# A two-layer attention kernel: an exponential released earlier, pieces of the MLP's input made between gelus, six first scores moved up

## The reference

```python
q = gconv1x1(bn1(x), qw); kv = grid_sample(bn1(x), grid + tanh(offsets(q)) * 4)      # 64 keys per head
bias = mlp3(sign(pos) * log1p(|pos|))                                              # 2 -> 64 -> 64 -> 1
x = x + conv1x1(softmax(q k^T * scale + bias) v, out_w) + out_b
x = x + conv1x1(gelu(conv1x1(bn2(x), mlp_w1) + mlp_b1), mlp_w2) + mlp_b2           # 256 -> 1024 -> 256
q, k, v = x W_qkv + b_qkv                                                          # second layer
x = x + softmax(q k^T * scale) v W_out + b_out                                     # 16 heads of 1024 x 1024
```

## Time and profile before

| | us |
|---|---|
| median of three runs (lowest, highest) | 1280.26 (1278.66, 1280.81) |
| the profiled execution's own time | 1279.23 |
| its span, first to last instruction | 1277.3 |
| PE busy | 1224.8 (96%) |
| DVE busy | 800.3 (63%) |
| ACT busy | 834.7 (65%) |
| POOL busy | 695.0 (54%) |

### The profile page before, as it was taken

How to read it: one execution, slowest core, us unless ns; L and a number is a source line. 1 busy time by engine, 2 the same in 40 slices (tenths; PEclk the granted TensorE clock), 3 DMA queues, 4 the chain that set the end, 5 groups by cost and what they waited for, 6 DMA issues and landing times.

```text
span 1277.3 us, 25474 instructions
## 1 busy us (share of the span) xinstructions
PE 1224.8 (96%) x10548; PEld 539.0 (42%) x10548; DVE 800.3 (63%) x1026; ACT 834.7 (65%) x1024; POOL 695.0 (54%) x391
## 2 busy tenths in 40 slices
PE   6499999999999999999999999898999899999998
PEld 4333333333333333333333333656886555555554
DVE  6766666666666666666666665554332677777773
ACT  4678777777777777887778877447442355555552
POOL 3366666666666666666666665250000056666664
PEclk9589999999999999999999999998999999999999
DMA  2340110111011011011001100000004413222212
GB/s 76 97 145 2 34 34 1 35 34 31 4 34 34 1 35 35 1 35 34 25 11 34 34 1 2 1 1 1 1 1 165 172 38 71 61 61 61 60 36 78
DMA packets 22507, 51.67 MB, mean 40 GB/s; under 512 B 5622, under 2 KB 10870, under 8 KB 22264
## 3 DMA queue, kind: packets, MB, share of 16 engines
q1 hardware_dynamic: 20084, 43.74, 12.2%
q10 hardware_dynamic: 2308, 6.30, 2.0%
HBM read 36.64 MB, written 11.15 MB: 37 GB/s over the span
## 4 chain that ended last, share of the span: by engine, by line
PE 90%; DVE 4%; ACT 2%; DMA 1%; POOL 1%; issue 1%; SPq 0%; POOLq 0%; DVEq 0%; ACTq 0%
PE ps L999 34%; PE ps L1008 18%; PE ps L1203 6%; PE ps L1233 5%; PE ps L990 5%; PE ps L1244 5%; PE ps L1136 4%; PE ps L1121 3%; PE ps L1165 2%; PE ps L1254 2%; PE ps L1298 1%; PE ps L1179 1%; DVE big L711 1%; PE ps L1021 1%; PE ps L1024 1%
## 5 line engine op out<-in xcount | busy, mean ns | idle before, releaser
L999 PE MATMUL ps<-big,w 64*64 64x512 f32 x2736 | 324.0, 590 | 0.0
L558 ACT ACTIVATE big<-ps 128x1024 f32<-128x1024 f32 x172 | 176.2, 1024 | 87.7 <-PE ps L999 87.7
L770 DVE TENSOR_SCALAR big<-big 128x1024 f32<-128x1024 f32 x171 | 118.7, 694 | 169.2 <-POOL big L447 169.2
L447 POOL TENSOR_TENSOR big<-qpad 128x1024 f32<-128x1024 f32 x86 | 164.3, 1911 | 96.6 <-DVE big L770 28.7
L764 DVE TENSOR_TENSOR big<-qpad,ps 128x1024 f32<-128x1024 f32 x171 | 207.4, 1213 | 1.2 <-PE ps L969 1.2
L447 POOL TENSOR_TENSOR big<-qpad,V 128x1024 f32<-128x1024 f32 x85 | 162.4, 1910 | 80.2 <-DVE ring L770 28.8
L558 ACT ACTIVATE big<-ps,vec 128x1024 f32<-128x1024 f32 x172 | 190.6, 1108 | 0.1
L863 DVE TENSOR_REDUCE amax<-ps 128x1 f32<-128x1024 f32 x128 | 154.0, 1210 | 43.2 <-PE ps L1203 42.4
L999 PEld LDWEIGHTS ps<-big,w 64*64 64x64 f32 x2736 | 98.0, 133 | 151.8 <-issue 85.5
L1008 PE MATMUL ps<-big,w3s 128*32 128x512 f32 x1376 | 160.4, 595 | 0.0
L999 PE MATMUL ps<-ring,w 64*64 64x512 f32 x1360 | 160.4, 588 | 0.0
(11 more groups left out here) (179 smaller groups left out, 1680.8 us busy)
## 6 DMA issues: line engine op xcount, KB each, us to landing
raw<-s_f SPq DMA_DIRECT2D x32, 512.0 KB, 5.9
h1l<-k_d SPq DMA_DIRECT2D x33, 128.0 KB, 3.6
h1h<-q_d ACTq DMA_DIRECT2D x33, 128.0 KB, 4.2
X<-in_x SPq DMA_DIRECT2D x2, 1024.0 KB, 6.1
q_d<-XN SPq DMA_DIRECT2D x4, 512.0 KB, 3.1
k_d<-XN SPq DMA_DIRECT2D x4, 512.0 KB, 3.4
q_d<-big SPq DMA_DIRECT2D x4, 512.0 KB, 3.6
k_d<-big SPq DMA_DIRECT2D x4, 512.0 KB, 3.8
```

Source lines behind the costliest of these rows:

```text
L447: pool.tensor_tensor(h1[m % HRING].rearrange("p (y a b) -> p y a b", y=2, b=W), u.unsqueeze(2).to_broadcast(shape), a[:, :, HALF // W * hf ...
L558: act.activation(h2[m % H2RING], z2[m % ZRING], ACT.Relu, bias=v("cb2") if m % 2 else 0.0).then_inc(h2_ready, 1)
L770: dve.tensor_scalar(h1[m % HRING], h1[m % HRING], 0.0, None, ALU.max).then_inc(h1_ready, 1)
L999: last = pe.matmul(z2[m % ZRING][CH * y:CH * (y + 1), HALF * x:HALF * (x + 1)], w2[CH * x:CH * (x + 1), :], h1[m % HRING][CH * x:CH * (x + ...
```

## The change

1. ACT's wait for the last burst moves from ahead of the loop over u to the copies of u = 2 to 9. The exponentials of u = 0 and 1 no longer wait for it.
2. ACT makes the pieces of block 0 of the MLP's input before the gelus, and those of block n + 1 before the third step of block n. DVE's `split_x` follows the same way: the two of block 0 between the additions to X, the two of block n + 1 ahead of the fourth step of block n.
3. `along(0)` to `along(5)` (`EARLY` = 6) move into `project3(5)` to `project3(7)`: one between the two halves, one behind the value. These six share one pair of PSUM banks, 4 and 5, so each waits for the maximum of the one before. Values use banks 6 and 7 alone. On DVE two maxima stand ahead of each remainder of n = 5 to 7. `along(6)` waits for the remainder of n = 6, `along(7)` for that of n = 7, and `value(8)` to `value(15)` stand between `along(6)` to `along(13)`.

```diff
+EARLY = 6
@@ along_pair
+            if x < EARLY:
+                return 2
@@ scalar
-            act.wait_ge(l3_done, PAIRS * G // BURST)
             for u in range(G + 2):
                 if 2 <= u < 10:
                     n = u - 2
+                    act.wait_ge(l3_done, PAIRS * G // BURST)
...
-            for n in range(T):
+            def normed_x(n):
                 for ct in range(CT):
...
+            normed_x(0)
             for i in range(T * FT):
                 f = i % FT
+                if f == 2 and i // FT < T - 1:
+                    normed_x(i // FT + 1)
                 act.wait_ge(hid_ready, i + 1)
...
             for n in range(NK, 2 * NK):
                 save_value(n)
-            max_high(0)
+                if turning(n - NK + EARLY):
+                    max_high(0)
@@ vector
-                    if r > 0:
-                        split_x(r - 1)
-            split_x(CT * T - 1)
+                    if r in (2, 3):
+                        split_x(r - 2)
...
             for i in range(T * FT):
+                if i % FT == 3 and i // FT < T - 1:
+                    for ct in range(CT):
+                        split_x(CT * (i // FT + 1) + ct)
...
             for n in range(2 * T):
+                for x in range(2 * (n - 2 * T) + EARLY, 2 * (n - 2 * T) + EARLY + 2):
+                    if x >= 0:
+                        maxes(x)
                 dve.wait_ge(f_hi, n + 1)
...
-                if x < SLOTS:
+                if EARLY <= x < SLOTS:
                     maxes(x)
@@ tensor, project3
+                early = 2 * (n - 2 * T) + EARLY
                 for hf in range(2):
                     for kt in range(CT):
...
+                    if hf == 0 and early >= 0:
+                        along(early)
                 last.then_inc(p_ready, 1)
+                value(n)
+                if early >= 0:
+                    along(early + 1)
@@ value
-                elif n >= 4:
-                    pe.wait_ge(vv_saved, n - 3)
+                elif n >= 2:
+                    pe.wait_ge(vv_saved, n - 1)
-                    last = pe.matmul(bank(4 + n % 4)[:, 0:C], ...
+                    last = pe.matmul(bank(6 + n % 2)[:, 0:C], ...
@@ along
-                if 2 <= x < AHEAD_MAX and not turning(x - 1):
+                if x == 0:
+                    pe.wait_ge(bo_saved, 1)
+                elif x < EARLY:
+                    pe.wait_ge(mx_ready, x)
+                elif x < EARLY + 2:
+                    pe.wait_ge(f_lo, 2 * T - (x == EARLY))
+                elif x < AHEAD_MAX and not turning(x - 1):
                     pe.wait_ge(mx_ready, x if turning(x) else x - 1)
@@ tensor, main
             for n in range(2 * T):
                 project3(n)
-                value(n)
-            pe.wait_ge(f_lo, 2 * T)
-            for x in range(AHEAD_MAX):
-                if x < NK:
-                    value(NK + x)
+            for x in range(EARLY, AHEAD_MAX):
+                value(NK + x - EARLY)
```

More of the change, by code:

```diff
@@ L621, in save_value @@
                 act.wait_ge(vv_ready, n + 1)
-                act.activation(V[:, NH * b:NH * (b + 1), jt, :], bank(4 + n % 4)[:, 0:C].rearrange("p (n d) -> p n d", d=D),
+                act.activation(V[:, NH * b:NH * (b + 1), jt, :], bank(6 + n % 2)[:, 0:C].rearrange("p (n d) -> p n d", d=D),
                                ACT.Identity).then_inc(vv_saved, 1)
@@ L1166, in project3 @@
                                          X[:, CT * b + kt, HALF * hf:HALF * (hf + 1)], start=(kt == 0), stop=(kt == CT - 1))
+                    if hf == 0 and early >= 0:
+                        along(early)
                 last.then_inc(p_ready, 1)
+                value(n)
+                if early >= 0:
+                    along(early + 1)
             def value(n):
                 b, jt = n // NK, n % NK
-                if n == 1:
-                    pe.wait_ge(bo_saved, 1)
-                elif n == 2:
+                if n == 0:
                     pe.wait_ge(x2_ready, CT * T)
-                elif n >= 4:
-                    pe.wait_ge(vv_saved, n - 3)
+                elif n >= 2:
+                    pe.wait_ge(vv_saved, n - 1)
                 for kt in range(CT):
-                    last = pe.matmul(bank(4 + n % 4)[:, 0:C], X[:, CT * b + kt, P * jt:P * (jt + 1)], wv[:, kt, 2, :],
+                    last = pe.matmul(bank(6 + n % 2)[:, 0:C], X[:, CT * b + kt, P * jt:P * (jt + 1)], wv[:, kt, 2, :],
                                      start=(kt == 0), stop=(kt == CT - 1))
@@ L1187, in along @@
                     pe.wait_ge(st_in[n % HEADS3], 96 * (n // HEADS3 + 1))
-                if 2 <= x < AHEAD_MAX and not turning(x - 1):
+                if x == 0:
[5 more added lines that the diff above has]
+                elif x < AHEAD_MAX and not turning(x - 1):
                     pe.wait_ge(mx_ready, x if turning(x) else x - 1)
-                elif 2 <= x < AHEAD_MAX:
+                elif x < AHEAD_MAX:
                     pe.wait_ge(m_lo, 1)
-                elif x < 2:
-                    pass
                 elif turning(x):
```

## The result

| | before | after |
|---|---|---|
| median of four runs side by side (us) | 1279.81 (1278.66 to 1280.81) | 1265.33 (1263.76 to 1267.42) |
| profiled execution, own time / span | 1279.23 / 1277.3 | 1263.76 / 1262.0 |

The ratio is 0.9888, 95% interval 0.9869 to 0.9908: 14.5 us faster, against a forecast of 1266.0.

A forecast was written before the change was run, and what follows sets the result against it. PE, on 90% of the span, was taken to lose time by waiting or running at its lower clock in three places. Gains 3.0 + 6.5 + 4.7 = 14.2 us gave a median of 1266.0, range 1262.5 to 1272.0.

The forecast's parts named there:

- Part 1: Last burst's end: earlier exponential removes PE's wait of 2.20 and the slow clock behind it; 3.0 us, bounds 2.2 and 3.9.
- the second head was late next: Behind the last burst: with the first wait gone, the second head's normalization comes at 811.7, 2.7 before the old 814.43.
- Part 2: Start of the MLP: pieces made between the gelus let `mlp_out(0)` follow `hidden(2)` without a wait; 6.5 us, bounds 3.6 and 6.5.
- both its terms: Start of the MLP: PE's wait of 3.56 us goes, and 2.94 of slow matmuls behind it if that wait lowered the clock.
- The room in front of `mlp_out(2)`: MLP's third step: delayed third gelu lets `mlp_out(2)` start at 880.3, PE comes at 880.4; 0.1 us of room.
- Part 3: Second attention's start: six early scores end the fourteenth maximum at 1018.9 instead of 1023.6; 4.7 us, bounds 3.0 and 5.9.
- The walk up to the first `across`: PE and DVE timed from `along(0)` at 990.0: last remainder ends at 1007.5, fourteenth maximum at 1018.9.
- the upper bound: First `across`, second attention: the early scores' upper bound of 5.9, with some 0.9 more if the clock level holds.
- The sum: Whole kernel: 3.0 + 6.5 + 4.7 = 14.2 us gained, giving a median of 1266.0.
- Rival C: Early scores gain nothing: head 0's operands land some 5 us later, or PE loses what DVE wins; 1270.7, chance 0.08.
- Rival D: Early scores: short PE waits drop the clock, 42.4 us for what takes 25.2; 1283.2, slower than before, chance 0.05.

The follow-up runs named there:

- the filled wait: Kernel before the change, with 14 extra matmuls whose result nobody reads put into PE's wait ahead of `mlp_out(0)`: 1276.61 us, ratio 0.9985.
- part 3 alone: Kernel before the change, with only the six early scores (`EARLY` = 6) and all that belongs to them: 1271.37 us, ratio 0.9948.
- head 0's loads earlier: Changed kernel with head 0's query loads issued behind n = 2, heads 1 and 2 behind n = 3 and 4: 1262.25 us, ratio 0.9866.
- the wait filled: Changed kernel with five extra matmuls in PE's wait of 1.41 us ahead of the first `across`: 1263.74 us, ratio 0.9874 to the kernel before.
- both: Changed kernel with head 0's query loads issued earlier and five extra matmuls ahead of `across(0)`: 1262.36 us, ratio 0.9865 to the kernel before.
- the loads split: Changed kernel with query loads issued one head at a time behind n = 3, 4 and 5, not all behind n = 3: 1263.90 us, ratio 0.9883.
- the changed kernel again: The changed kernel unaltered, timed once more on another chip: 1265.92 us, ratio 0.9902 to the kernel before.

## Why the prediction was right, and which term was mis-sized

**Part 1** was put at 3.0 and measured 3.30. The wait went, the clock stayed up, and the second head was late next, when the prediction had it: its normalization ended at 811.33 + 1.04 - 0.70 = 811.67 by the clock of before, put at 811.7.

```profile
811.33 1.04 POOL L464 TENSOR_TENSOR ring<-ring,srec 128x512 f32<-128x512 f32 x1 [3.38 <-DVE srec L819]
```

The 0.3 more lie behind it. The transposes of the second and the third head started, before and after (the second of after, 812.42, is shown above), at

```profile
814.23 1.06 PE L1097 MATMUL ps<-ident,ring 128*128 128x128 f32 x4
...
817.29 0.60 PE L1097 MATMUL ps<-ident,ring 128*128 128x128 f32 x4
```

```profile
814.68 0.60 PE L1110 MATMUL ps<-ident,ring 128*128 128x128 f32 x4
```

Counted from the burst, the second came 2.51 sooner and the third 3.31. So the matmuls between them, which ran partly at the lower level before, gave 0.80, where the prediction had added 0.3 to 2.7.

**Part 2** was put at 6.5 and measured 6.52, and both its terms separately by the filled wait. The room in front of `mlp_out(2)`, put at 0.1, was 0.69 less a handover of some 0.15, since ACT's instructions, back to back, start every 0.71 and 0.57 us, not every 0.80 and 0.69.

**Part 3** is the mis-sized term: 4.7, measured 4.94 + 1.40. The walk up to the first `across` held. Shifted by the 9.12 by which `project3(0)` came sooner, it had `along(1)` at 984.6 (985.08), the last remainder's end at 998.4 (998.80), the fourteenth maximum at 1009.8 (1009.55). What it left out was the clock behind: the earlier trace rows show the first `across` at 1.19, and the prediction put a clock that holds into the upper bound, at 0.9, rather than into the sum. (4.7 + 0.9 is 5.6, not the 5.9 given; 0.3 of that bound has no source.) The trace of the kernel before shows where that clock fell, with PE ahead of the first `across` and then three stretches (columns as above):

```profile
1015.19 0.73 PE L1203 MATMUL ps<-h1l,h1h 96*128 96x512 f32 x2 [0.53 <-DVE amax L863]
1016.41 0.27 PE L1214 MATMUL ps<-ident,amax 128*8 128x128 f32 x1 [0.49 <-DVE amax L863]
1017.45 2.07 PE L1203 MATMUL ps<-h1l,h1h 96*128 96x512 f32 x4 [0.77 <-DVE amax L863]
```

```profile
1016.00:1018.00 2.00, 0.82 (x2) 0.58 (x3) 1.58 (x3) 1.26 (x2) 0.00 (x0) 0.86 0.00 0
1018.00:1020.00 2.00, 1.53 (x5) 0.67 (x3) 1.29 (x2) 0.28 (x1) 0.00 (x0) 0.50 0.02 4
...
1023.75:1030.00 6.25, 5.99 (x20) 4.00 (x21) 3.58 (x3) 3.59 (x6) 2.14 (x1) 0.69 0.01 3
```

It fell while PE waited for single maxima, ahead of the wait of 1.41. With six maxima done early these short waits are gone but for one of 0.34. The clock then held, and gave 1.40, in executions like the first profiled one; in others it falls at the wait of 1.41, and the median lies between.

**The sum.** In the profiled execution the stages gained 16.0 against 14.2. That the median came within 0.7 of the forecast is partly luck: the executions in which the clock falls at `across(0)`, which the prediction didn't foresee, took back part of what it had put too low.

**Rival C** fell with part 3 alone. Its fear of a late operand was real in a small way: `along(0)` waited for head 0's queries in three of the profiles, for 0.3 to 1.2 us. **Rival D** named a mechanism that exists, at another place and size. The prediction noted that no row shows a series of short waits; the trace of the kernel before has one, in the lines just above, with the clock at 0.50 behind it, and D's chance of 0.05 left that out. The early scores' waits (1.13, 0.31 and 0.34 us) left the clock at 1.00. The one ahead of `across(0)` sometimes doesn't, and that costs 2.6 us, not 17: the stretch at the lower level was some 6.8 us long there, where D reckoned with 42. The Trainium skill ("TensorE: Matmul & The Clock Gate", A second HAM failure mode: psum-queue depth-cycling) says that short idles of PE between groups of matmuls can make the clock swing and cost throughput. This case's trace agrees for the kernel before (0.50 behind 0.53, 0.49 and 0.77 us) and for the wait of 1.41 in one of the changed kernel's three profiles (0.52 against 1.00), and disagrees for the early scores' waits.

**What stays open:** why the clock falls at the wait ahead of `across(0)` in about half of the executions. One profile of the changed kernel shows the fall; for the other runs it is read from their mean clock alone. That clock stayed at 0.986 in all twelve runs with head 0's loads earlier, the wait filled, or both, but also in the four with the loads split, whose profile has 1.23 us of waiting at `along(0)` and the 1.41 as well. So no run shows whether an earlier wait takes part, and four runs with the filled wait alone are few against a rate of one half. Open too are the longest runs: 1269.05 of the changed kernel, 1275.00 and 1275.48 of part 3 alone lie 4.6 to 6.0 us above the shortest of the same kernel, more than 2.6, and none of them was profiled.

## What to carry to other kernels

Price a wait of PE twice: its length, and what runs at half the clock behind it; filling it with idle matmuls, which moves no real work, measures the second part alone. When work is moved into an earlier stage, follow its operands there too: here the loads' issue on ACT and their landing among other transfers, which had held PE up by 0.4 us at most with the old order of scores, set the pace, and issuing them one tile earlier was worth 1.4 us more in the trace. A spread of several us within one kernel is worth a second profile: 2.6 us of it was a single stretch at the lower clock.

## What the runs showed of the hardware that was not expected

- Issuing nine loads of 128 KB from ACT kept it from its next activation for 6.0 us in one execution and 7.3 in another, while the DMA engines were busy at a share of 0.8 to 1.1 in most microseconds; single issues took 0.32 to 1.9 us.
- Head 0's third query load, issued at 975.8 to 975.9 into those busy engines, landed 3.9 us later in the first profile and 6.1 and 6.3 us later in two others (the changed kernel again, the loads split). Issued at 971.0 and 971.5, ahead of them, it was not waited for (head 0's loads earlier, both).
- PE's clock was 1.00 behind a wait of 1.41 us in one profile and fell in another with the same waits, to the tenth of a microsecond, ahead of it. In the kernel before it was at 0.50 behind three waits of 0.49 to 0.77 us.
